# GpSimd's indirect fetches and scatters tied to the progress of the attention and the feed-forward, in a two-block vision network with a graph-attention router on one core

## What is computed

```python
x = x + L0_conv(ln(x))      # attention in 8x8 tiles: 64 tiles an image, 8 heads; the 64 queries of a
                            # tile see 12x12 keys, with relative positions; softmax; projection
t = t + L0_ffn(ln(t))       # 2047 of an image's 4096 positions, chosen by a learned weight, go through
                            # gelu(x@w1+b1)@w2+b2; the others pass unchanged
x = x + L1_conv(ln(x))      # dilated attention over 3x3 taps, dilations 2 and 3
t = t + L1_ffn(ln(t))       # a graph attention over 524288 random edges gives each of 16384 nodes
                            # scores; its two best of 4 experts are mixed
```

## Time and profile before

| what | us |
|---|---|
| median of 3 runs | 7381.07 |
| lowest and highest of them | 7369.02 and 7398.86 |
| the profiled execution's own time | 7399.85 |
| its span, first to last instruction | 7397.9 |
| TensorE matmul busy | 3084.1 (42%) |
| VectorE busy | 3409.7 (46%) |
| ScalarE busy | 1538.9 (21%) |
| GpSimd busy | 2602.1 (35%) |

### The profile page before, as it was taken

The page is one execution under the profiler, slowest core; times in us unless marked ns, Lnnn a source line. Parts: engine busy times, 40 slices in busy tenths (PEclk is TensorE's granted clock), DMA queues, the critical chain, the costliest instruction groups (busy, mean ns, idle before and its releaser), DMA issues.

```text
span 7397.9 us, 84797 instructions
## 1 busy us (share of the span) xinstructions
PE 3084.1 (42%) x32140; PEld 1902.7 (26%) x32141; DVE 3409.7 (46%) x6941; ACT 1538.9 (21%) x3954; POOL 2602.1 (35%) x2472
## 2 busy tenths in 40 slices
PE   0011117687887798738874122222222222222205
PEld 0011106553773485226722000000000000000104
DVE  9999935757766685726665011111111111111128
ACT  0000005421651274016510011111111111111100
POOL 0000051100000000040001777777777777777450
PEclk9965558886997698658975555555565655555556
DMA  2000023000100100010002122222222222222207
GB/s 78 0 0 0 0 68 116 25 1 23 16 2 1 37 4 1 0 27 3 2 1 39 16 32 37 32 38 32 32 32 32 32 32 32 32 32 32 62 7 244
DMA packets 259708, 227.82 MB, mean 31 GB/s; under 512 B 115005, under 2 KB 222954, under 8 KB 250282
## 3 DMA queue, kind: packets, MB, share of 16 engines
q0 software_dynamic: 78944, 29.28, 6.3%
q1 hardware_dynamic: 99786, 99.91, 4.4%
q10 hardware_dynamic: 80640, 93.86, 4.1%
HBM read 100.42 MB, written 121.39 MB: 30 GB/s over the span
## 4 chain that ended last, share of the span: by engine, by line
PE 26%; another core or an unknown queue 23%; issue 18%; DVE 17%; DVEq 6%; ACT 4%; DMA 3%; POOL 2%; ACTq 1%; SPq 0%; POOLq 0%
DVE SA_ L1305 3%; PE PSB L382 2%; PE PSB L679 2%; DVE SA_ L1295 2%; PE PSB L1157 2%; PE PSB L661 2%; PE PSB L527 2%; PE PSB L352 2%; POOL VPAD L958 2%; DVEq L1386 1%; PE PSB L392 1%; DVE SA_ L583 1%; PE PSB L516 1%; PE PSB L366 1%
## 5 line engine op out<-in xcount | busy, mean ns | idle before, releaser
L948 POOL DMA_INDIRECT SA_<-s_T,GIX x2048 | 2186.6, 1068 | 659.0 <-issue 659.0
L1157 PE MATMUL PSB<-VPAD,EH 128*128 128x512 f32 x512 | 299.4, 748 | 1995.6 <-DMA VPAD<-s_TNT 1562.0
L940 POOL DMA_INDIRECT s_AEXP<-fill,SIX x128 | 139.2, 1087 | 2467.4 <-DMA fill<-s_ADT 2426.3
L897 DVE TENSOR_TENSOR XPAD<-SA_ 128x256 f32<-128x256 f32 x32 | 14.2, 444 | 1830.3 <-DMA SA_<-s_T,GIX 1830.3
L1157 PEld LDWEIGHTS PSB<-VPAD,EH 128*128 128x128 f32 x512 | 120.6, 245 | 2195.3 <-DMA VPAD<-s_TNT 1603.6
L1161 PE MATMUL PSB<-SA_,EW 128*128 128x512 f32 x512 | 346.3, 825 | 345.2 <-ACT SA_ L1142 198.6
L849 POOL DMA_INDIRECT SA_<-s_SK,BLKI x128 | 121.0, 945 | 1018.5 <-DVE BLKI L1438 976.9
L303 ACT ACTIVATE PRX<-PSB,MX 128x144 f32<-128x144 f32 x1024 | 375.3, 380 | 337.2 <-DVE MX L224 337.0
L1409 PE MATMUL PSB<-ident,SA_ 128*128 128x128 f32 x448 | 81.8, 364 | 838.0 <-DVE SA_ L1376 576.7
L1146 ACT ACTIVATE VPAD<-PSB,PRX 128x512 f32<-128x512 f32 x128 | 87.9, 687 | 1308.4 <-remote 941.7
L1142 ACT ACTIVATE SA_<-PSB,PRX 128x512 f32<-128x512 f32 x256 | 175.9, 687 | 773.7 <-remote 432.4
(11 more groups left out here) (365 smaller groups left out, 7536.3 us busy)
## 6 DMA issues: line engine op xcount, KB each, us to landing
SA_<-s_T,GIX POOLq DMA_INDIRECT x2048
s_Y<-VPAD ACTq DMA_DIRECT2D x32, 1024.0 KB
s_R<-zero SPq DMA_DIRECT2D x96, 256.0 KB
s_R<-XPAD ACTq DMA_DIRECT2D x32, 768.0 KB
SB_<-s_Y SPq DMA_DIRECT2D x16, 1024.0 KB, 5.4
SA_<-s_Y SPq DMA_DIRECT2D x16, 1024.0 KB, 7.3
s_AEXP<-zero SPq DMA_DIRECT2D x32, 256.0 KB, 3.0
SA_<-in_x SPq DMA_DIRECT2D x16, 512.0 KB
```

Of the source, the lines that this page charges most:

```text
L948: pool.indirect_dma_start(out=n.G[:,s,c,:],out_offset=None,in_=d["T"],in_offset=IOA(ap=n.GIX[s][:,c:c+1],axis=0)).then_inc(n.gath[s],16)
L1157: pe.matmul(PSB[:,(m%4)*512:(m%4+1)*512],n.WM1[:,m//2,(m%2)*P:(m%2+1)*P],n.TNC[:,s,:],start=True,stop=True).then_inc(n.moe_h,1)
```

## The change

Waits are put between the calls of three groups. Nothing else is changed.

- Key blocks (128 calls): the first 8 go at once. From then on a pair of calls waits for the tile `t//2-3` of the first attention, so that one pair goes with each tile; the last pair waits for tile 60 of 64.
- Keys (32 calls): the first 4 go at once, and then each waits for one more product `s_h` of the first feed-forward.
- Scatters (the 96 of image 3): the first 8 go at once, and then a pair goes with each tile of image 3's attention (64*(IMGS-1) is the count of `s_ao` at its start); the last pair waits for tile 44. The 32 scatters after image 3 stay as they were.

```diff
     for t in range(NT):
+        if t%2==0 and t>=8: pool.wait_ge(n.s_ao,t//2-3)
         pool.indirect_dma_start(out=I[:,t*BLK:(t+1)*BLK],out_offset=None,in_=d["SK"],in_offset=IOA(ap=m.BLKI[:,t:t+1],axis=0)).then_inc(n.gb_ld,16)
     pool.wait_ge(n.end_rdy,1)
     rows=d["SK"].rearrange("(r a) c -> r (a c)",a=2)
     for t in range(BLOCKS):
+        if t>=4: pool.wait_ge(n.s_h,t-3)
         pool.indirect_dma_start(out=I[:,t*128:(t+1)*128],out_offset=None,in_=rows,in_offset=IOA(ap=m.QI[:,t:t+1],axis=0)).then_inc(n.a2_ld,16)
...
     for t in range(NT):
         if t==0: pool.wait_ge(n.np_rdy,1); pool.wait_ge(n.ad_ld,16)
         if t==NT-NT//IMGS: pool.wait_ge(n.ad_ld2,16)
+        if t%2==0 and 8<=t<NT-NT//IMGS: pool.wait_ge(n.s_ao,64*(IMGS-1)+t//2-3)
         pool.indirect_dma_start(out=d["AEXP"],out_offset=IOA(ap=n.SIX[:,t:t+1],axis=0),in_=n.ADN[:,t,:],in_offset=None,bounds_check=4096*128-1,oob_is_err=False).then_inc(n.ad_sc,16)
```

## The result

The changed kernel takes **7330.33 us** (median of 11 executions, 7310.25 to 7358.88), the kernel before on the same chip 7382.43 us (11 executions, 7365.77 to 7407.17). The ratio is 0.9926, with a 95% interval of 0.9909 to 0.9943: 52 us or 0.7% faster. 7205 us was forecast, 176 us less than before.

The account below looks back on a forecast made before the run. Back-to-back GpSimd calls were taken to hold other engines, TensorE above all, 1.4 us each. Stalls -297, pairs +104, single calls +10, first calls +7 gave -176 us: 7205 us from the 7381 median, range 7110 to 7390.

Parts of the forecast that it names:

- The stalls come from the calls; 297 us are at stake.: Images 0 and 3: 297 us are lost beside 256 GpSimd calls, and spacing the calls removes these stalls.
- the calls are not the cause: Rival: what stalls the images merely runs at the same times as the calls; 7381 us, chance 0.03.
- The starts of images 0 and 3 and the feed-forward come free.: Excess before the tiles and in image 0's first feed-forward goes: 137.9, 18.5 and 34.3 us.
- The 28 single key fetches: Spaced calls in the first feed-forward, beside large matmuls: 0.35 us each, 10 us added.
- the first calls of each group: Calls that still go at once: 4.1 us in image 3 and about 3 us in image 0, 7 us added.
- I take 1.0 us a pair.: Attention tiles of images 0 and 3: each pair of calls costs 1.0 us, 104 us for 104 pairs.
- the 6 us that were named as the sign of being wrong: Tiles with pairs were to take 4.3 to 5.3 us; 6 us or more would show the prediction wrong.
- the first 8 scatters: Start of image 3: 48 matmuls took 4.8 us instead of 0.7, read as 4.1 us for 8 calls, 1.0 a pair.
- A pair is over before much fills up.: In a tile, room for some tens of TensorE instructions must fill first, and the next tile empties it.
- a pair costs in full: Rival: calls cost the same 1.4 us each wherever they stand, so spacing only spreads the loss; 7365 to 7425, chance 0.14.
- The clock.: TensorE's granted clock in the tiles stays near 0.99; the rival said it falls, giving 7444 us, chance 0.12.
- the 102.5 us wait: VectorE's wait before tile 1's maximum in image 3, 102.52 us, was to be gone after the change.

Follow-up runs that it names:

- all_later: Changed kernel with fetches after the first 8, key fetches and image 3's scatters moved from the tiles into feed-forwards and second layers: 7075.11 us, ratio 0.9588.
- The lone call: Changed kernel plus one unused gather a tile, in image 1 released by `s_ao`, in image 2 by `s_mx`: 7380.78 us.
- scatter_later: Changed kernel with image 3's 96 scatters moved from its tiles into its feed-forward and second layer: 6836.5 us, ratio 0.9988.
- singles_shifted: Changed kernel with image 0's two calls a tile released apart, by `s_ao` and `s_mx`, and image 3's pairs by `s_mx`: 6813.65 us.
- sitting 1: First group of follow-up runs, in which the calls hold almost nobody; the kernel before took 6847.97 us.

## Why the prediction was wrong, step by step

- **The stalls come from the calls; 297 us are at stake.** Right. all_later gives 7384.68 - 7075.11 = 310 us. The rival "the calls are not the cause" falls. The Trainium skill, SBUF — State Buffer, Who interferes with whom, says that only the port pair shared by VectorE and GpSimd causes contention; as a forecast for these calls the runs disagree with it: SBUF ports may be free, but 60 pairs cost 147 us.
- **The starts of images 0 and 3 and the feed-forward come free.** Right: -144.6, -17.8 and -32.5 us. The 28 single key fetches cost 1.7 us, where 10 were taken, and the first calls of each group nothing, where 7 were taken: image 0 reaches its first maximum in 26.5 us and image 3 in 33.9, image 1 without calls in 33.3.
- **"I take 1.0 us a pair."** This step failed. The pair costs 2.4 to 2.5 us, and 104 pairs 255 us instead of 104. With it the sum is -297 + 255 + 2 = -40 us, near the measured 52; the tiles with pairs take 6.2 us, beyond the 6 us that were named as the sign of being wrong. The value was taken from the first 8 scatters of image 3, by how late TensorE's matmuls came. The runs showed two errors in that. First, the matmul rows do not show all of the hold: in the first tile above the 48 matmuls take 1.06 us, and VectorE gets them 2.16 us later, and so it is in 38 of 60 tiles of image 0. In image 3 most of the hold does stand in the rows, but with 3.2 us from the first score to the end of the last in the tile shown, where 0.7 is the length without calls. Second, the 4.1 us were divided by 8 calls, though only 4 of them fell between 3234.09 and 3238.86: the fifth starts at 3234.28, just behind the first score (it was not yet running when TensorE got there, as the working has it), and the eighth at 3238.11. By those 4 it is 1.0 us a call and 2.1 a pair, near what came. The other four went out ahead of the scores, while image 3 was prepared, and held nothing that shows. A mean over such moments is no price for pairs that go by `s_ao`, the one moment after which TensorE's next signal is what everybody waits for. The lone call shows it: 0.84 us there, 0.03 us behind `s_mx`. So do the ten pairs of image 3 in the changed kernel that came behind the scores.
- **"A pair is over before much fills up."** Wrong. A pair is over after 2 x 1.4 us, and the signal, or the last of the matmuls, comes after it.
- **The rival "a pair costs in full"** was nearly what happened, with its own reason (`s_ao` fires just as the scores are issued), at 2.2 to 2.5 us where it gave 2.4 to 2.8. The case against it, the first 8 scatters, was the reading that misled. It was given 0.14. Its total of 7365 and more lies above the measured 7330, since it also charged the 28 single calls 1.41 us each; they cost 0.06.
- **The clock.** 0.99 was expected, 0.86 and 0.79 came. It adds to the price and is not its core. In image 0 of the changed kernel 26 of the 60 tiles with pairs lie wholly at the upper level (2.4 GHz) and take 5.91 us in the mean, 2.1 more than a tile without calls (3.8); all 60 together take 6.2, 2.4 more. So some 0.3 us of the 2.4 go with the clock. In image 3 it is more: 9 tiles at the upper level with a pair that started before the scores were over take 5.1 to 7.0 us, the 5 at the lower level 8.1 us in the mean. This compares tiles of one execution; no run changes the clock alone, and the shares stay estimates. With the lone calls at `s_ao` the tiles lose 0.84 us at a clock of 0.98.
- **What came as forecast in the profile, and what did not.** Right: the 102.5 us wait is gone, and the tiles of image 3 behind the last pair are back near 3.8 us (65 us for the last 17). Wrong, beside the size of the tiles: the pairs of image 0 stand 1.77 us apart, not 1.25 (1203.93 and 1205.70), while those of image 3 keep 1.28, and images 1 and 2, which were not to move, are 18 us shorter in their second layers, at a higher clock and without a call of their own.

What stays open is what in the chip delays the signal. The runs show that it is the indirect form (not GpSimd's memset, not its plain DMA), the call (not its rows), 1.4 us of each, and TensorE's instructions and signals; which path they share, no view shows.

## What to carry to other kernels

- Before spacing calls, look for the handoff that ends last in the loop, and release each call right after it, not right before. 60 calls, one for a tile, cost 50 us behind one semaphore and 2 us behind another that comes 1.7 us earlier in the loop; as 60 pairs at the first they cost 147 us.
- Price such a wait by the signal (consumer's start less producer's end), not by the producer's rows. An engine whose rows look nearly untouched can still be what everybody waits for. Look at more than one tile: here some show the hold in the rows and some do not.
- Loops of few large matmuls (here the feed-forward and the second layer, 120 calls for nothing) are the place for indirect calls when the loop of many small ones has no slack.

## What the runs showed of the hardware

- The same program with the same inputs took 7382 to 7393 us in four sittings and 6836 to 6848 in two, with the executions of a sitting within 0.7% of each other. In the two short ones a call of the edges' loop takes 1.28 us instead of 1.39, and a pair at `s_ao` costs 0.1 us (image 0 of scatter_later: (246.8 - 238.6)/60 = 0.14). In the long ones, too, GpSimd issues the back-to-back fetches and scatters ahead of the loop every 1.27 and 1.28 us; the others are held all the same. This is no property of one chip for good: of the two sittings that name the same chip, one took 6836 and one 7386 us.
- Held are TensorE's instructions and the signals from it, not those between the others, as far as one tile shows. In the kernel before, amid the back-to-back scatters, a maximum that had waited 24.68 us ends at 3257.81 + 0.76 = 3258.57, ScalarE takes it at 3258.60, and TensorE takes ScalarE's last exponential (end 3260.16) at 3260.21:

```profile
3258.60 0.38 ACT L303 ACTIVATE PRX<-PSB,MX 128x144 f32<-128x144 f32 x1 [22.80 <-DVE MX L224]
...
3259.95 0.21 ACT L303 ACTIVATION_READ_ACCUMULATOR PRX<-PSB,MX 128x1 f32 x1
...
3260.21 0.52 PE L363 MATMUL PSB<-SB_,QW 32*64 32x144 f32 x4 [21.35 <-ACT PRX L303]
```

- The row of a block fetch is often 1.46 us instead of 0.94 when it meets the score matmuls (line 850 after, first call of a pair). This is no sign of the hold: in singles_shifted of sitting 1, where the calls hold almost nobody, 56 of the 128 rows are as long, while the scatters of image 3's pairs after mostly keep 0.97 us and cost as much.
